# Two score banks as one pair: products issued two by two, both row maxima in one VectorE instruction

## The reference

```
scores = jnp.einsum('bhqd,bhkd->bhqk', q, k) * SCALE
attn = jax.nn.softmax(scores, axis=-1)
out = jnp.einsum('bhqk,bhkd->bhqd', attn, v)
```

## Time and profile before

| what | value |
|---|---|
| median of the runs | 2325.64 us |
| the profiled execution | 2323.41 us |
| its span, first to last instruction | 2321.4 us |
| TensorE (PE) busy | 2018.8 us, 87% |
| VectorE (DVE) busy | 1572.5 us, 68% |
| ScalarE (ACT) busy | 1235.4 us, 53% |
| mean granted TensorE clock | 0.950 of full speed |

### The profile page before, as it was taken

One profiled execution on the slowest core, in us unless ns is written; L12 is line 12 of the kernel. 1 busy time (PEld: TensorE's weight loads), 2 busy tenths in 40 slices (PEclk: granted clock), 3 DMA queues, 4 the chain that ended last, 5 costly groups with the idle time before them and its releaser, 6 DMA issues. The chain is left out here.

```text
span 2321.4 us, 49821 instructions
## 1 busy us (share of the span) xinstructions
PE 2018.8 (87%) x13328; PEld 1154.5 (50%) x13329; DVE 1572.5 (68%) x4268; ACT 1235.4 (53%) x2600; POOL 924.3 (40%) x958
## 2 busy tenths in 40 slices
PE   4789999898998998999989998884139999999997
PEld 2343443344443444444444443232128988888885
DVE  4477888887887888788787889973264444444443
ACT  0246666565665556656566566663145554545553
POOL 2222233433333234232342334333146666666653
PEclk9899999999999999999999999997569999999999
DMA  2312322223232223222232322310243333333331
GB/s 88 101 56 69 97 74 80 83 73 82 74 88 75 77 76 88 75 83 75 70 89 73 86 75 79 79 34 28 100 159 65 64 63 63 62 63 62 63 59 22
DMA packets 171886, 172.31 MB, mean 74 GB/s; under 512 B 30786, under 2 KB 160404, under 8 KB 171668
## 3 DMA queue, kind: packets, MB, share of 16 engines
q1 hardware_dynamic: 141396, 134.87, 20.1%
q0 software_dynamic: 30272, 34.80, 9.3%
HBM read 100.70 MB, written 68.99 MB: 73 GB/s over the span
## 5 line engine op out<-in xcount | busy, mean ns | idle before, releaser
L1162 DVE TENSOR_REDUCE mxs<-bank 128x1 f32<-128x512 f32 x1024 | 696.6, 684 | 218.1 <-PE bank L503 198.8
L833 ACT ACTIVATE pt<-bank 128x512 f32<-128x512 f32 x1024 | 588.5, 594 | 371.4 <-PE bank L512 368.2
L503 PE MATMUL bank<-ks,qs 96*128 96x512 bf16 x1024 | 400.2, 392 | 80.0 <-DVE mxs L1162 60.3
L512 PE MATMUL bank<-qs,ks 99*128 99x512 bf16 x1024 | 395.2, 387 | 9.8 <-ACT pt L833 9.2
L1780 PE MATMUL bank<-xh,gu_h 128*128 128x256 bf16 (+1 forms) x1152 | 309.6, 269 | 3.6 <-issue 1.9
L1780 PE MATMUL bank<-xl,gu_h 128*128 128x256 bf16 (+1 forms) x1152 | 308.4, 268 | 0.0
L1780 PE MATMUL bank<-xh,gu_l 128*128 128x256 bf16 (+1 forms) x1152 | 308.2, 268 | 0.0
L1740 POOL DMA_INDIRECT out<-y_sb,ids x136 | 217.2, 1597 | 203.2 <-ACT y_sb L1831 178.7
L521 PE MATMUL bank<-pt,v_sb 128*32 128x512 f32 x2048 | 279.5, 619 | 0.0
L503 PEld LDWEIGHTS bank<-ks,qs 96*128 96x128 bf16 x1024 | 103.7, 101 | 349.7 <-DVE mxs L1162 234.0
L1888 DVE TENSOR_TENSOR hid_e<-bank,act_g 128x256 f32<-128x256 f32 (+1 forms) x288 | 116.9, 406 | 170.0 <-PE bank L1780 166.5
(11 more groups left out here) (290 smaller groups left out, 3443.5 us busy)
## 6 DMA issues: line engine op xcount, KB each, us to landing
qs<-qk_dram SPq DMA_DIRECT2D x128, 128.0 KB, 2.6
ks<-qk_dram SPq DMA_DIRECT2D x64, 192.0 KB, 3.3
xt<-x_t SPq DMA_DIRECT2D x16, 512.0 KB, 3.9
h_dram<-h_sb SPq DMA_DIRECT2D x16, 512.0 KB, 3.5
qs<-qk_dram SPq DMA_DIRECT2D x128, 64.0 KB, 2.3
ks<-qk_dram SPq DMA_DIRECT2D x64, 128.0 KB, 3.3
hw<-h_dram SPq DMA_DIRECT2D x16, 512.0 KB, 4.2
out<-hw SPq DMA_DIRECT2D x16, 512.0 KB, 3.0
```

The lines of the kernel that those rows point to most:

```text
L503: mm(score[u % 2][:, :], qs[0:QK, h, blk(t)], ks[0:QK, h, :], start=True, stop=True) \
L512: mm(scoret[u % 2][:, :], ks[0:QK + MROWS, h, blk(t)], qs[0:QK + MROWS, h, :], start=True, stop=True).then_inc(s("pe_st"), 1)
L833: f(pt[:, t % 2, j, :], scoret[u % 2][:, :], ACT.Exp).then_inc(s("act_exp"), 1)
L1162: v.reduce_max(mxs[:, t, g * GH + j:g * GH + j + 1], score[u % 2][:, :], AX.X).then_inc(s("dve_mx"), 1)
```

## The change

Banks 0 and 1 become one tensor `pair` of two banks. At even units only, TensorE waits until all earlier pairs of maxima are done and then issues the score products of units u and u + 1, which signal once. VectorE takes both maxima at the even unit in one reduction over a 128x2x512 operand with two results per partition. The counts of the two semaphores are halved. All else stays where it was.

```diff
@@ vit_layer
-        banks = [outer.enter_context(nc.psum_tensor(f"bank{k}", [128, 512], F32)) for k in range(8)]
+        pair = outer.enter_context(nc.psum_tensor("bank_pair", [128, 2, 512], F32))
+        banks = [pair[:, k, :] for k in range(2)]
+        banks += [outer.enter_context(nc.psum_tensor(f"bank{k}", [128, 512], F32)) for k in range(2, 8)]
...
@@ tensor_program
         def score_unit(b, g, u):
-            j, t = u // TB, u % TB
             if u == 0:
                 wait(pe, s(f"stacked{g}"), 16 * len(Q_STACK + K_STACK), b, 16 * len(Q_STACK + K_STACK))
-            wait(pe, s("dve_mx"), UNITS * NG, b, UNITS * g + u - 1)
-            h = g * GH + j
-            mm(score[u % 2][:, :], qs[0:QK, h, blk(t)], ks[0:QK, h, :], start=True, stop=True) \
-                .then_inc(s("pe_a"), 1)
+            wait(pe, s("dve_mx"), UNITS // 2 * NG, b, UNITS // 2 * g + u // 2)
+            h = g * GH + u // TB
+            for k in range(2):
+                last = mm(score[k][:, :], qs[0:QK, h, blk(u % TB + k)], ks[0:QK, h, :], start=True, stop=True)
+            last.then_inc(s("pe_a"), 1)
 
         def scoret_unit(b, g, u):
             t, j = u // GH, u % GH
@@ -529,7 +531,7 @@
                         T, P, C, W, X = fresh(pe, UNITS * g + u, T, P, C, W, X)
                         st, tg, mt = in_slot(g, P, C, W)
                     at = UNITS * g + u
-                    if C.ok:
+                    if C.ok and u % 2 == 0:
                         score_unit(C, g, u)
                     if st[0].ok:
                         scoret_unit(*st, u)
@@ -1158,12 +1160,12 @@
 
         def head_max(b, g, u):
             j, t = u // TB, u % TB
-            wait(dve, s("pe_a"), UNITS * NG, b, UNITS * g + u + 1)
-            v.reduce_max(mxs[:, t, g * GH + j:g * GH + j + 1], score[u % 2][:, :], AX.X).then_inc(s("dve_mx"), 1)
+            wait(dve, s("pe_a"), UNITS // 2 * NG, b, UNITS // 2 * g + u // 2 + 1)
+            v.reduce_max(mxs[:, t:t + 2, g * GH + j], pair[:, :, :], AX.X).then_inc(s("dve_mx"), 1)
 
         def negate_maxima(b, g):
 
-            wait(dve, s("dve_mx"), UNITS * NG, b, UNITS * (g + 1))
+            wait(dve, s("dve_mx"), UNITS // 2 * NG, b, UNITS // 2 * (g + 1))
             ch = Link("dve_chain_m", NG * 4, b, 4 * g)
             hs = heads(g)
             scl = scs[:, b.par, 0:TB * NH].rearrange("p (t h) -> p t h", t=TB)[:, :, hs]
```

More of the change, by code:

```diff
@@ L142, in vit_layer @@
         tile_expert = sb("tile_expert", [1, tiles], I32)
-        banks = [outer.enter_context(nc.psum_tensor(f"bank{k}", [128, 512], F32)) for k in range(8)]
+        pair = outer.enter_context(nc.psum_tensor("bank_pair", [128, 2, 512], F32))
+        banks = [pair[:, k, :] for k in range(2)]
+        banks += [outer.enter_context(nc.psum_tensor(f"bank{k}", [128, 512], F32)) for k in range(2, 8)]
         programs = token_phase(nc, outer, images, x_t, cls, w0_t, w1_t, wo_t, attn_w_t, gate_w, consts, out,
-                               h_dram, qk_dram, x2_dram, list_dram, cst, tile_row, tile_expert, banks, total)
+                               h_dram, qk_dram, x2_dram, list_dram, cst, tile_row, tile_expert, pair, banks, total)
         with ExitStack() as inner:
@@ L151, in token_phase @@
 def token_phase(nc, outer, images, x_t, cls, w0_t, w1_t, wo_t, attn_w_t, gate_w, consts, out,
-                h_dram, qk_dram, x2_dram, list_dram, cst, tile_row, tile_expert, banks, total):
+                h_dram, qk_dram, x2_dram, list_dram, cst, tile_row, tile_expert, pair, banks, total):
     tokens, cap, big, tiles, list_rows = geometry(images)
```

## The result

The changed kernel takes 2386.63 us (median of 4 runs, 2380.92 to 2392.09) beside 2325.86 us of the kernel before on the same chip: ratio 1.0261, 95% interval 1.0239 to 1.0284. That is 61 us slower; forecast were 2352 us, 28 more than before, with a range that ended at 2385. The profiled execution took 2380.92 us, span 2378.9 against 2321.4.

What follows compares the result with a forecast made beforehand. TensorE and VectorE, both nearly full, were taken to hold each other up in turn. Terms of 1.0 + 0.6 + 0.4 = +2.0 us an image, over 14 images' worth, gave +28 us: 2352 us, range 2312 to 2385.

Steps and rivals of the forecast that it cites:

- the price of the pair: One VectorE maximum over both banks, 1024 columns, was taken to cost 1.22 us.
- the term for the images at both ends: First and last two images lack part of the overlapped work; all images counted as 14 images' worth of +2.0 us, +28.
- The turnaround itself is mostly covered: Every pair: turnaround of 1.92 us fits in 2.97 us per pair; only even-unit work for which TensorE waits at once costs.
- the remaining places: L608 at unit 3 a little later, an exponential at unit 6 a little earlier: counted at 0 together.
- L657's other three cases at nothing: The transposes come four times an image; three cases counted at nothing because VectorE's odd-unit work before them comes earlier.
- units 24 to 29: Projection L781 at unit 29 waits for VectorE's L1438 of unit 28, no slack: +0.6 us an image.
- Units 8 to 11: Weighting delays transposes L657 at unit 9 by 0.75 us, then L1421 delays L552 at unit 11: sum +1.0 us an image.
- Units 50 to 63: Behind the payload, idle before S53 goes but VectorE's chain sets the end: bounds -2.3 to +1.9, taken +0.4 us an image.
- more before S54 and S56: Sign of being right: TensorE idles more before the score products of units 54 and 56, and not before S53.
- The clock: Rival: longer waits at units 9 and 29 and before S56 and S62 pull the clock down, adding 24 us: 2376; chance 0.15.
- the waits just vanish: Rival: TensorE no longer waits at odd units where VectorE is late, half its idle goes: 2300 us; chance 0.2.
- The pair is no cheaper: Rival: the pair costs 1.37 us like two maxima, +0.15 us at two places, 4 us in all; inside the range.

Runs made afterwards that it cites:

- after_half: Changed kernel with each maximum over 256 of the 512 scores of a row, order and release unchanged: 2283.4 us, ratio 0.982.
- The four moves: Changed kernel with weighting, class token's output (h2c), second query part and bound operands each hung one unit earlier on VectorE: 2336.2 us, ratio 1.0037.
- after_scatter_later: Changed kernel with three of an image's eight GpSimd scatters issued at units 61 to 63, behind GpSimd's block of unit 60: 2366.9 us, ratio 1.0195.
- after_moved_scatter: Changed kernel with four VectorE pieces hung one unit earlier and three of eight scatters put behind GpSimd's block of unit 60: 2305.7 us, ratio 0.9934.
- the later scatters: Three of eight GpSimd scatters put behind its block of unit 60; in the kernel before, alone: 2321.7 us, 0.9978; in the changed kernel: 2366.9 us, 1.0195.
- the twin without it: Kernel before, without the pair, with the same four VectorE pieces one unit earlier and three scatters behind GpSimd's block of unit 60: 2315.3 us, ratio 0.9956.
- the pair's order with two separate maxima: Both products and two 512-column maxima at the even unit, banks released singly, with four pieces one unit earlier and three scatters later: 2302.2 us, ratio 0.9895.

## Why the prediction fell short

Right were the direction, the price of the pair, and its mechanism: even-unit work behind two maxima, for which TensorE waits at once. L659 and L783 stand where the working put them, and the idle before S53 is gone.

Wrong was the size, and two terms of the sum failed. By the profiled executions 57.5 us came where the sum had 28.

The larger miss is the term for the images at both ends, "with the first and last two images, which lack part of the overlapped work, 14 images' worth": the sum had 6 us for these five, and 24 came, 18 of the missing 30. It took their loss for smaller because less is overlapped there; but what the other images overlap is what covers the pair's turnaround, and where that is missing it is bare. "The turnaround itself is mostly covered" failed there. In the first image TensorE's own idle before a score product for a maximum rose from 4.6 to 10.2 us. The first image, before and after (us, engines' busy time, clock):

```profile
101.90:177.80 75.90, 66.76 (x300) 28.76 (x300) 56.62 (x134) 33.62 (x66) 16.07 (x19) 0.91 0.31 82
```

```profile
101.10:184.80 83.70, 68.50 (x300) 28.63 (x302) 56.55 (x108) 33.83 (x67) 16.02 (x18) 0.86 0.29 77
```

TensorE's idle in all rises from 9.1 to 15.2 us. In after_half the first image takes 75.3 us, 8.4 less: what the shorter instruction saves at 16 of the image's 32 pairs. The four moves give back 12 of the 16.5 us of images 0 to 2, so the pieces behind the pair are in this loss too.

The other miss, 12 us in the eleven images, is the step that counts "the remaining places" at "0 together", with those that it did not name at all. They are:
- *Units 0 to 7*, +1.46 us an image, 16 us in eleven. I saw L608 at unit 3 and gave it nothing; I didn't follow GpSimd's chain from the payload, which the change delays, over the scatters to L600 of the next image. after_scatter_later and after_moved_scatter show it.
- *Units 38 to 49*, +0.66: at unit 44 the pair stands behind a VectorE piece and TensorE has lost the lead that covered it.
- *L657's other three cases at nothing*: the case at unit 24 costs 0.39 us. With 0.75 at unit 28 and 0.27 given back at unit 26, units 24 to 29 came to 0.87 for 0.6. Units 8 to 11 came to 1.32 for 1.0.

Units 50 to 63 were sized too dear: -1.18 us for +0.4, inside the bounds of -2.3 to +1.9. The choice near the upper half was wrong: the sign "more before S54 and S56" did not come, for in the image shown S54 waits 0.15 us and S56 nothing, and only S62 waits longer. But GpSimd's operand takes the gain back at unit 1.

The clock was priced as a rival and came in part. At units 0 to 3 it was low in ten of eleven images, before in six, and 9.6 us went to slower matmuls there; over the whole stage the mean went from 0.98 to 0.97 only. Time at the lower of the two levels does half the work, so these means over the eleven images' 1045.9 and 1080.0 us stand for an estimated 21 and 32 us lost, some 11 more of their 34; no run changes the clock alone, so that this share is on the path is argued and not shown. The Trainium skill, "TensorE: Matmul & The Clock Gate", section "A second HAM failure mode: psum-queue depth-cycling", tells of a kernel that cycled through PSUM banks with brief idles of TensorE, and whose clock swung between its two levels and cost throughput. The trace agrees that more idle and more time at the low clock come together: at units 0 to 3, where 9.6 us, about a sixth of the whole loss, went that way. That the idle is the cause no run here shows.

Of the rivals, "the waits just vanish" fell with L659, which waits longer. The wait before S53 did vanish, 1.2 us an image at units 52 and 53, and was outweighed elsewhere. "The pair is no cheaper" fell with the 1224 ns.

The last image and the end took 5.4 us longer after the change, all of it in the image's 64 units (74.7 us from its first score product to its last maximum before, 80.3 after). Not settled is why the program behind the last maximum is shorter with the later scatters (757 to 760 us in those profiles, 762 to 767 in the others), with the pair or without it; no run here tells.

## What to carry to other kernels

Merging two instructions of an engine that isn't the last saved nothing here and moved a release: ask at every place of the period, across its end into the next one and over the third engine too, what stands behind the merged instruction and who waits, and count the places by cutting its length rather than by the waits that show already. A pair of buffers released as a whole takes the producer's lead away, which is what covered the consumer's other work, and the beginning and end of a pipeline, where least is overlapped, can lose most. When an order changes, what stood right behind the changed instruction has to move with it: here the four moves turned 2.6% slower into 0.4% slower, and with the later scatters 0.7% faster, while the same in the kernel before gives 0.4% slower and 0.4% faster. So the gain of these versions is not shown to be the change's; over the twin without it only the pair's order with two separate maxima is faster, by 0.6%.

## What the runs showed of the hardware

Across two banks the maximum took 691 ns for 512 columns in two runs of 256 and 1224 for 1024, so 533 ns for 512 more; in one bank 512 columns took 684, so the step from one bank to the next cost 7 ns at most in the mean. GpSimd's fixed finish was not expected: eight scatters of 0.96 to 1.08 us each and what stands between them end the operand of unit 1 at the same 21.5 us after S50 in ten of eleven images. With three scatters fewer ahead of it it ended at 18.3, and the program took 15 us less, 5 of which the kernel before gained by them too.
